# Attention of the chosen tokens: the order of the small steps in a query tile, Wo in four pieces, one subtraction on GpSimd

## What is computed

```python
hn = rmsnorm(x_sel, ln1)
q = rope(heads(hn @ wq), pos_sel); kk = rope(heads(hn @ wk), pos_sel); v = heads(hn @ wv)
sc = einsum('bhqd,bhkd->bhqk', q, kk) / sqrt(hd) + m_sel[:, None]
a = softmax(sc, axis=-1)
o = einsum('bhqk,bhkd->bhqd', a, v).reshape(b, kc, d) @ wo
x1 = x_sel + o
x2 = x1 + gelu(rmsnorm(x1, ln2) @ w1) @ w2
```

## Time and profile before

| | |
|---|---|
| time, median of 3 runs | 1944.22 us (1940.25 to 1946.42) |
| the profiled execution | 1945.36 us, of which the span from first to last instruction is 1943.6 us |
| busy, share of the span | PE 95%, DVE 74%, ACT 45%, POOL 8% |
| granted TensorE clock, mean | 0.985 |
| attention stage | from about 1404 to 1745 us |

### The profile page before, as it was taken

How to read it: one execution, slowest core, us unless ns; L and a number is a source line. 1 busy time by engine, 2 the same in 40 slices (tenths; PEclk the granted TensorE clock), 3 DMA queues, 4 the chain that set the end, 5 groups by cost and what they waited for, 6 DMA issues and landing times. The chain is left out here.

```text
span 1943.6 us, 72290 instructions
## 1 busy us (share of the span) xinstructions
PE 1848.5 (95%) x32348; PEld 1567.1 (81%) x32348; DVE 1445.2 (74%) x3477; ACT 875.7 (45%) x1494; POOL 148.7 (8%) x179
## 2 busy tenths in 40 slices
PE   6999999999999999999999999879899999879998
PEld 5888888888888888888888888657677777667997
DVE  6888788888887777787777777667588788876222
ACT  4443334343434443444434343325588787764110
POOL 2000000000000000000000000041100000001000
PEclk9999999999999999999999999879999999999999
DMA  4111211121121112111111110236500000015000
GB/s 147 47 46 58 73 52 46 58 74 52 46 74 52 36 36 61 43 36 40 59 41 36 47 51 30 95 95 183 164 26 12 13 12 23 13 41 161 17 12 22
DMA packets 65139, 108.45 MB, mean 56 GB/s; under 512 B 4720, under 2 KB 25216, under 8 KB 64832
## 3 DMA queue, kind: packets, MB, share of 16 engines
q1 hardware_dynamic: 59056, 84.69, 14.0%
q0 software_dynamic: 5776, 19.15, 3.2%
HBM read 59.26 MB, written 27.26 MB: 45 GB/s over the span
## 5 line engine op out<-in xcount | busy, mean ns | idle before, releaser
L1083 PE MATMUL proj<-xnT_high,held 128*128 128x256 f32 x1536 | 235.2, 288 | 3.3 <-DVE xnT_low L782 2.4
L1083 PEld LDWEIGHTS proj<-xnT_high,held 128*128 128x128 f32 x1536 | 203.6, 191 | 9.2 <-DVE xnT_low L782 2.9
L444 POOL TENSOR_TENSOR xs<-xs 128x512 f32<-128x512 f32 x63 | 80.9, 1285 | 1170.0 <-DVE xs L885 1170.0
L1083 PE MATMUL proj<-xnT_low,held 128*128 128x256 f32 x1024 | 163.7, 281 | 0.0
L2088 DVE CUSTOM_DVE_ANT_0 Sm<-Sp,held 128x1023 f32<-128x1023 f32 x128 | 155.5, 1216 | 8.0 <-DVE xs L2076 2.0
L1986 ACT ACTIVATE Sm<-Sm,least 128x1023 f32<-128x1023 f32 x128 | 146.7, 1146 | 14.1 <-DVE least L2088 13.3
L1083 PEld LDWEIGHTS proj<-xnT_low,held 128*128 128x128 f32 x1024 | 140.1, 190 | 0.0
L2141 PE MATMUL Sp<-KS,held 128*128 128x512 f32 x256 | 94.4, 451 | 29.9 <-DVE least L2088 25.6
L506 ACT ACTIVATE Pq<-Pq 128x1024 f32<-128x1024 f32 x63 | 66.9, 1062 | 123.4 <-DVE Pq L848 123.3
L486 ACT ACTIVATE QT<-proj 128x512 f32<-128x512 f32 x64 | 38.1, 595 | 182.4 <-PE proj L1083 182.4
L2038 DVE COPY PTs<-Tp 128x512 f32<-128x512 f32 x128 | 88.3, 690 | 29.7 <-PE Tp L2153 29.2
(11 more groups left out here) (343 smaller groups left out, 4341.2 us busy)
## 6 DMA issues: line engine op xcount, KB each, us to landing
VS<-DV SPq DMA_DIRECT2D x64, 264.0 KB, 3.9
xs<-in_x SPq DMA_DIRECT2D x32, 512.0 KB, 4.8
out_rows<-xs SPq DMA_DIRECT2D x64, 256.0 KB, 2.0
mask_columns<-x1T SPq DMA_DIRECT2D x16, 512.0 KB, 5.2
xs<-in_w SPq DMA_DIRECT2D x16, 512.0 KB, 3.8
xe<-in_x SPq DMA_DIRECT2D x15, 512.0 KB, 3.5
QT<-in_wqT SPq DMA_DIRECT2D x1, 1024.0 KB, 6.5
KT<-in_wkT SPq DMA_DIRECT2D x1, 1024.0 KB, 9.4
```

Of the source, the lines that this page charges most:

```text
L444: pool.tensor_tensor(Ass[k], T1s[k], T2s[k], ALU.add).then_inc(s_as, 1)
L1083: ins = pe.matmul(bank[:, g * BT:g * BT + BT], w[hw][:, c, o:o + P], xnT[hx][:, c, :], start=n + c == 0, stop=n == 2 and c == G - 1)
```

## The change

It moves steps in the hand-written lists and splits two of them. The arithmetic is the same.

- PTs becomes two rings, one for each half of the key blocks, so that ACT's copies and DVE's copies wait each for their own half of the product with V; each half of `values` signals s_pv, and the second alone waits for DVE's copy.
- `project` is issued as four pieces at heads 8, 9, 11 and 12 instead of at once at head 8.
- The low part of the query stack is computed by GpSimd, and ACT's high part moves from head 0 to head 4. PE's stacks for the next tile move from heads 10 to 13 to heads 7 and 15 and to heads 0 and 1 of the next tile, and ACT's copies with them.
- DVE's `attention_rows` moves from head 5, behind the copy, to head 4, ahead of the copy. `second_norm` moves from heads 9, 10, 13 and 14 to heads 13, 14 and 15 and to head 0 of the tile after; `norm_t` moves from head 15 to head 2 of the tile after.
- ACT's copy of a turned half comes before its other copies of the same pass.

```diff
@@ -1866,8 +1866,11 @@
             least = sb("least", [P, 4], c=c2_)
...
             rinv = sb("rinv", [P, H], c=c2_)
-            SLOTS = 5
-            PTs = sb("PTs", [P, SLOTS, Q, P], c=c2_)
+            QH = Q // 2
+            SLOTS = (5, 5)
+            PIECES = (range(0, QH), range(QH, Q))
+            PARTS = len(PIECES)
+            PTs = [sb(f"PTs{e}", [P, SLOTS[e], QH, P], c=c2_) for e in range(2)]
             OTs = sb("OTs", [P, G, P], c=c2_)
...
             OnT = sb("OnT", [P, G, P], c=c2_)
@@ -1908,14 +1911,14 @@
             s_keep = sem("s_keep", c2_)
             KC = K - 1
-            def slot(t, h):
-                return (t * H + h) % SLOTS
-
-            def read_before(eng, t, h):
-
-                n = t * H + h - SLOTS
+            def slot(t, h, e):
+                return (t * H + h) % SLOTS[e]
+
+            def read_before(eng, t, h, e):
+
+                n = t * H + h - SLOTS[e]
                 if n >= 0:
-                    eng.wait_ge(s_pv, n // 4 + 1)
+                    eng.wait_ge(s_pv, n // 4 * PARTS + 1 + e)
             def tile(t):
...
+                    pool.wait_ge(s_qh, t + 1)
+                    pool.tensor_tensor(qst[:, :, 2:4, :], q_rows(t), qst[:, :, 0:2, :].bitcast(F32),
+                                       ALU.subtract).then_inc(s_ql, 1)
                 for b in range(2):
                     pool.wait_ge(s_mg[b], 16 * (Q // 2))
-
-            def q_rows(t):
-                return qrow[:, tile(t), :].rearrange("p o (h d) -> p h o d", d=DK).broadcast_to([P, H, 2, DK])
             @block.scalar
...
                     act.wait_ge(s_t, t * (2 * H) + (2 * h + 1))
-                    read_before(act, t, h)
-                    act.activation(PTs[:, slot(t, h), 0:4, :], Tp[0][:, :].rearrange("p (k q) -> p k q", k=4),
+                    read_before(act, t, h, 0)
+                    act.activation(PTs[0][:, slot(t, h, 0), :, :], Tp[0][:, :].rearrange("p (k q) -> p k q", k=4),
                                    ACT.Copy).then_inc(s_ta, 1)
                 def take_o(t, g):
-                    act.wait_ge(s_pv, t * G + (g + 1))
+                    act.wait_ge(s_pv, PARTS * (t * G + g + 1))
                     act.activation(OTs[:, g, :], Op[:, 0:P], ACT.Copy).then_inc(s_oc, 1)
                 def stack(t):
@@ -1985,22 +1991,26 @@
                         act.wait_ge(s_sm, t * H + (h + 2))
...
                                        scale=-1.0, accum_out=rsum[:, b, h:h + 1]).then_inc(s_e, 1)
+                        if h > 0:
+                            take_t(t, h - 1)
+                        elif before:
+                            take_t(t - 1, H - 1)
                         if h == 2 and before:
...
                             take_o(t, h // 4 - 1)
-                        if h > 0:
-                            take_t(t, h - 1)
-                        elif before:
-                            take_t(t - 1, H - 1)
-                        if h == 1 and before and t >= 2:
+                        if h < 2 and before:
+                            take_stack(t, h + 2)
+                        if h == 2 and t >= 2:
                             take_x1(t - 2)
-                        if h == 7 and before:
+                        if h == 4 and after:
+                            stack(t + 1)
+                        if h == 6 and before:
                             take_on(t - 1)
-                        if h == 0 and after:
-                            stack(t + 1)
-                        if 10 <= h < 14 and after:
-                            take_stack(t + 1, h - 10)
+                        if h == 7 and after:
+                            take_stack(t + 1, 0)
+                        if h == 15 and after:
+                            take_stack(t + 1, 1)
                 act.sem_inc(s_ta, 1)
                 act.sem_inc(s_oc, 1)
@@ -2034,15 +2044,9 @@
                 def take_t(t, h):
                     dve.wait_ge(s_t, t * (2 * H) + (2 * h + 2))
-                    read_before(dve, t, h)
-                    dve.tensor_copy(PTs[:, slot(t, h), 4:8, :], Tp[1][:, :].rearrange("p (k q) -> p k q", k=4))\
+                    read_before(dve, t, h, 1)
+                    dve.tensor_copy(PTs[1][:, slot(t, h, 1), :, :], Tp[1][:, :].rearrange("p (k q) -> p k q", k=4))\
                        .then_inc(s_td, 1)
-
-                def stack(t):
-                    dve.wait_ge(s_qh, t + 1)
-                    alone(dve, s_alone)
-                    dve.tensor_tensor(qst[:, :, 2:4, :], q_rows(t), qst[:, :, 0:2, :].bitcast(F32),
-                                      ALU.subtract).then_inc(s_ql, 1)
                 def weights(t, b):
                     dve.wait_ge(s_e, t * H + H)
@@ -2088,26 +2092,27 @@
                         dve.tensor_tensor_reduce(Sm[:, h % 4, 0:KC], Sp[h % 2][:, 0:KC], mc[:, b, 0:KC], 1.0,
...
                            .then_inc(s_sm, 1)
+                        if h == 4 and before:
+                            attention_rows(t - 1)
                         if h > 1:
...
                                 weights(t - 1, 1 - b)
-                        if h == 2 and after:
-                            stack(t + 1)
-                        if h == 5 and before:
-                            attention_rows(t - 1)
-                        if h == 9 and before:
+                        if h == 0 and t >= 2:
+                            second_norm(t - 2, 3)
+                            second_norm(t - 2, 4)
+                        if h == 13 and before:
                             second_norm(t - 1, 0)
-                        if h == 10 and before:
+                        if h == 14 and before:
                             second_norm(t - 1, 1)
-                        if h == 13 and before:
+                        if h == 15 and before:
                             second_norm(t - 1, 2)
-                            second_norm(t - 1, 3)
-                        if h == 14 and before:
-                            second_norm(t - 1, 4)
-                        if not after and (h < Q - 2 or h == 13):
+                            if not after:
+                                second_norm(t - 1, 3)
+                                second_norm(t - 1, 4)
+                        if not after and (h < Q - 2 or h == 14):
                             keep(min(h, Q - 2))
                 dve.sem_inc(s_sm, 1)
@@ -2157,22 +2162,25 @@
                 def values(t, g, part):
                     if part == 0:
+                        pe.wait_ge(s_oc, t * G + (g + 1))
                         pe.wait_ge(s_ta, t * H + (4 * g + 5))
+                    if part == 1:
                         pe.wait_ge(s_td, t * H + (4 * g + 5))
-                        pe.wait_ge(s_oc, t * G + (g + 1))
-                    for k in range(part * (Q // 2), (part + 1) * (Q // 2)):
+                    for k in PIECES[part]:
+                        e = k // QH
                         n = P if k < Q - 1 else P - 1
...
                             ins = pe.matmul(Op[DK * j:DK * j + DK, 0:P], V[0:n, k, h * DK:h * DK + DK],
-                                            PTs[0:n, slot(t, h), k, :], start=k == 0, stop=k == Q - 1)
-                    if part == 1:
-                        ins.then_inc(s_pv, 1)
+                                            PTs[e][0:n, slot(t, h, e), k % QH, :], start=k == 0, stop=k == Q - 1)
+                    ins.then_inc(s_pv, 1)
                 def back(t):
                     pe.wait_ge(s_oc, t * G + (G + 1))
-                    if t:
+                    if t > 0:
                         pe.wait_ge(s_x1, t)
+                    else:
+                        pe.wait_ge(s_qs, 2 * G)
                     for g in range(G):
...
                     ins.then_inc(s_on, 1)
@@ -2183,12 +2191,16 @@
                         ins = pe.transpose(Wp[:, g * P:g * P + P], On[:, g * P:g * P + P], ident[:, :])
                     ins.then_inc(s_ot, 1)
-                def project(t):
-                    pe.wait_ge(s_w, 16)
-                    pe.wait_ge(s_otc, t + 1)
-                    for g in range(G):
+                def project(t, gs):
+                    if gs[0] == 0:
+                        pe.wait_ge(s_w, 16)
+                        pe.wait_ge(s_otc, t + 1)
+                        if t < Q - 2:
+                            pe.wait_ge(s_qs, (t + 2) * G + 1)
+                    for g in gs:
                         ins = pe.matmul(Wp[:, :], OnT[:, g, :], wo[:, g, :], start=g == 0, stop=g == G - 1)
-                    ins.then_inc(s_wo, 1)
+                    if gs[-1] == G - 1:
+                        ins.then_inc(s_wo, 1)
                 def norm_t(t, stacks=False):
                     pe.wait_ge(s_h2, t + 1)
@@ -2198,13 +2210,14 @@
                         ins = pe.transpose(Wp[:, g * P:g * P + P], h2[:, g * P:g * P + P], ident[:, :])
                     ins.then_inc(s_h2t, 1)
```

(44 more changed lines are left out.)

## The result

| | before | after |
|---|---|---|
| median of 7 runs | 1942.03 us | 1952.38 us |
| range | 1940.07 to 1948.08 | 1950.08 to 1955.77 |
| profiled span | 1943.6 us | 1950.6 us |

The account below looks back on a forecast made before the run. With three engines near full, the order of their work was taken to bound the kernel. Tile 0 -2.0, tile 1 -0.3, tiles 2 to 6 +6.8, tile 7 +0.9 gave +5.4 us: 1950.5 us, range 1942 to 1960.

Parts of the forecast that it names:

- Two rules between the engines: Score comes 1.37 us after DVE's minimum starts; DVE's copy waits for the previous slot's turn; 4.75 us per two slots, heavy first.
- The walk: Slot-by-slot sum, 42.73 us per middle tile; slot h runs from PE's score of head h+2 to h+3, S(h) its start.
- Slots 3 and 4, +1.04: Moved attention_rows waits for `back` ahead of the copy; slots 3 to 6 lose 1.04 us a tile.
- Slots 14 to 2, +3.1: Second-norm steps in light slots make PE wait for DVE: 15.5 us from S(14) to S(3) instead of 12.4.
- Slots 7 to 13, -2.8: Wo in pieces of 0.84 us, with stacks and DVE's norm steps moved away, gains 2.75 us a tile.
- rival B: Each Wo piece leaves its own tail: 4 x 0.23 us more a tile, +6.4 us, 1957 us; 17%.
- C: Low ends: Wo pieces at 0.76 us, no ACT wait, 0.1 from the halves; -3.5 us, 1947 us; 15%.
- rival D: GpSimd's low part is late for PE's stack, beyond 3.9 us of cover; at 7.5 us an operation 1957.5 us; 5%.
- D2: GpSimd is late once, in tile 0, by a slow first call; at 8.5 us costs 2 us, 1952.5 us; 1%.
- Rival A: DVE carries a lead over the tile's end, covering the norm's pieces: -3.6 us a tile, 1932.8 us; 10%.
- E: ACT's moved copies of stack and x1 delay turns: +0.3 us a tile, 1952.5 us; counted with the forecast, together 52%.
- tile 7, +0.9 us: Last tile, with `keep` pieces and norm steps on DVE: first MLP product 54.7 us behind S(0) instead of 53.79.

Follow-up runs that it names:

- experiment 1: Changed kernel with DVE's attention_rows back at head 5, behind the copy: 1944.1 us, ratio 1.0008 to the kernel before.
- experiment 2: Changed kernel with the second norm's Newton steps and scaling moved from heads 15 and 0 to heads 1 and 2: 1944.3 us, ratio 0.9997 to before.
- experiment 3: Changed kernel with Wo in one piece again at head 8: 1959.4 us, ratio 1.0079 to the kernel before.
- experiment 5: Changed kernel with the low part of the query stack on VectorE again, at head 6: 1952.9 us, ratio 1.0052 to the kernel before.
- experiment 6: Kernel before with only the low part of the query stack moved to GpSimd: 1940.0 us, ratio 0.9978 to the kernel before.
- experiment 10: New order by the walk's rules, keeping GpSimd's low part, Wo in two pieces, other steps moved: 1934.6 us, ratio 0.9952 to the kernel before.
- experiment 4: Changed kernel with the first half of each product with V waiting for both copies again: 1951.8 us, ratio 1.0040 to the kernel before.
- experiment 7: Changed kernel with GpSimd's subtraction made twice, one after the other: 1950.0 us in its one run.
- experiment 9: Changed kernel with useless transposes in the last tile's slot 0, slot 4 and ahead of head 14's turn: 1949.5 us, ratio 1.0031 to before.
- experiment 8: Changed kernel with useless last-tile transposes in slot 0 and behind head 15's pass: 1951.4 us, ratio 1.0036 to the kernel before.

## Why the prediction held, point by point

- *Two rules between the engines bound a slot, not a sum of busy time.* Shown. The walk gave 42.73 us a tile and the chip took 42.73; slot by slot it is off by more than 0.1 us only in slots 8 to 13, where the records shift. Experiments 1, 2, 3, 5 and 6 changed single parts and experiment 10 the whole order, and the tile followed by 0.8, 1.6, 1.2, 0.1, 0.4 and 1.1 us (said: 1.0, 1.3 to 1.6, 1.4, 0.4 to 0.5, 0.4, 0.9 to 1.2). Busy time alone would have given nothing in experiments 1 and 2. What moved less than said in 1 and 5 was held by a step of ScalarE's that lay under the one that moved.
- *Slots 3 and 4, +1.04.* The size was right (2.81 for 1.82); undone it gives back 0.81, because ScalarE's 0.2 us lies under it (experiment 1).
- *Slots 14 to 2, +3.1.* Right: it lies in slots 14, 15 and 0 (3.55, 3.08 and 2.99); experiment 2 gives 1.6 back by moving the steps to heads with products.
- *Slots 7 to 13, -2.8.* Right (-2.8 by the table), with the pieces at 0.84 each and no tail of their own: rival B falls, tiles would be 43.6, and so does C with its lower ends, tiles would be under 42.3. Against Wo in one piece the split is worth 1.23 us (experiment 3); the other 1.5 us is there with Wo in one piece too, so it comes with the stacks and VectorE's steps that left these slots.
- *Halves of the products, 0.* Right: 0.04 for the wait (experiment 4). That the slots of PTs come free half by half was not tried alone.
- *GpSimd.* Its operation took 2.4 us (2.5 said), done at S(3) + 7.5 (7.6 said), and it has cover for a second one (experiment 7), so rival D falls, and D2 too: tile 0's first operation took 2.40 us like the others. What it is worth depends on the slot it leaves: 0.44 us a tile in the old order (experiment 6), 0.11 in the new (experiment 5), of 1.13 us of work.
- *Rival A, a lead of VectorE.* Falls: the waits in slots 14, 15 and 0 stood in full. *E*, 0.3 us a tile more by ScalarE, did not come either: the tile is the walk's.
- *Tiles 0 and 1:* -1.8 and -0.15 us in these two profiles (said -2.0 and -0.3). Tile 0 took 37.5 us here and 37.5 to 38.2 in the other variants with the same tile 0, so its gain is 1.2 to 1.8 us. *Tiles 2 to 6:* +6.75 (said +6.8).
- *The step that was mis-sized is tile 7, +0.9 us:* it measured +4.3 in the profiled execution, and the MLP behind it, taken as unchanged, +1.5 (199.15 against 197.68 us). I had added vector's steps by their durations at the full clock and never asked what idle times of 2.57, 2.17 and 2.23 us of TensorE do to the clock. With fillers in these gaps the tail is 55.2 us (+1.4, experiment 9), and without them 56.0 to 58.1 (the table there): in the profile of after about 2.9 us of the 4.3 go with the clock, in that of experiment 4, the same order, 0.7. The MLP's 1.5 us is not tied to the order: it was 197.65 to 197.8 us in eight of the ten variants, all with the same code for the MLP, at a granted clock of 0.97 over its first 60 us, as before; in the three profiles where it took longer (after, experiments 1 and 10: 198.5 to 199.15) that clock was 0.94. So the sum's +5.4 became 8.7 us in the timed runs (1.0045), between the walk at a full clock and the 10.5 of the profiled execution.
- *The time itself came out nearer than the sum.* 1950.5 was said and 1952.4 measured, but that is in part luck: 1950.5 stands on a median of 1944.2 us from three executions and one profile of 1945.4. From the median of seven, 1942.0, the same +5.4 gives 1947.4, 5 us short.

What stays open: why the same idle time of 2.57 us in slot 0 was followed by a lower clock in five profiles and not in experiment 4, and that of 2.17 us in slot 4 in after and experiments 7 and 8 and not in 3, 4 and 5. Each kernel has one profile, and no run here varied the idle time alone in steps.

## What to carry to other kernels

In a hand-written order, walk one period slot by slot with start-to-start distances from the trace and the few waits that couple the engines: work is free only where the partner engine has longer work beside it, and a step of 0.6 us in a slot without such cover costs all of it, while taking 1.1 us away in a slot that another rule binds gives 0.1 to 0.4. Move steps into the slots with cover; splitting a long block helps, while moving its followers to bare slots can cost more than the split brings. Where a new order opens idle times on TensorE as wide as the 2.2 to 2.6 us here, look there for a lower granted clock and count what follows at that clock.

## What the runs showed of the hardware

- Fillers that do nothing but keep TensorE occupied gave a tail of 55.2 us at a clock of 1.00 throughout, in one profile. Without them it was 56.0 to 58.1 us in seven kernels that fill at most one of the idle times, with the clock down in one to three places (0.66, 0.70 and 0.58 in after's stretches).
- The same idle time of 2.57 us did not always cost the clock (0.66 in after, 1.00 in experiment 4): two kernels that differ in one wait, worth 0.04 us a tile, had tails of 58.07 and 55.95 us in their profiles. An idle time of 2.23 us near the end was followed by a lower clock in all eight profiles that have it.
- GpSimd's 128x1024 subtraction took 2.38 to 2.40 us beside busy VectorE, and vector's minimum of 1.22 us beside it was as long as without it. The Trainium skill (GPSIMD Engine Reference, 1. Specifications) says the two share SBUF interfaces, with contention for vector instructions in a 2-port perf mode or with two SBUF inputs; the minimum here reads one input from PSUM, and no run tested one with two.
